# Cross-channel attention on one core: ten instead of eight batches loaded turned, with their loads and the small products placed anew

## What is computed

```python
rgb = jnp.transpose(rgb_emb, (0, 2, 1))      # x:   16 batches of 128 channels x 1024 positions
geo = jnp.transpose(geo_emb, (0, 2, 1))      # ctx: the same
scale = d ** (-0.5)                          # 8 heads of d = 16
def heads(x, w):
    return (x @ w.T).reshape(b, n, H, d).transpose(0, 2, 1, 3)
def xca(q, k, v):
    attn = jax.nn.softmax(jnp.einsum('bhni,bhnj->bhij', q, k) * scale, axis=-1)
    out = jnp.einsum('bhnd,bhde->bhne', v, attn)
    return out.transpose(0, 2, 1, 3).reshape(b, n, c)
res_p2r = xca(heads(rgb, wq_rgb), heads(geo, wk_point), heads(geo, wv_point)) @ proj_p2r.T
res_r2p = xca(heads(geo, wq_point), heads(rgb, wk_rgb), heads(rgb, wv_rgb)) @ proj_r2p.T
return jnp.transpose(rgb + res_p2r, (0, 2, 1)) + jnp.transpose(geo + res_r2p, (0, 2, 1))
```

## Time and profile before

| what | value |
|---|---|
| time, median of 3 runs | 140.67 us (140.2 to 141.71) |
| the profiled execution | 139.92 us, of which 137.9 us are the span of the trace |
| PE busy | 123.4 us (90%) |
| ACT busy | 86.1 us (62%) |
| POOL busy | 77.2 us (56%) |
| DVE busy | 71.3 us (52%) |
| moved by DMA | 34.25 MB |

### The profile page before, as it was taken

How to read it: one execution, slowest core, us unless ns; L and a number is a source line. 1 busy time by engine, 2 the same in 40 slices (tenths; PEclk the granted TensorE clock), 3 DMA queues, 4 the chain that set the end, 5 groups by cost and what they waited for, 6 DMA issues and landing times.

```text
span 137.9 us, 2676 instructions
## 1 busy us (share of the span) xinstructions
PE 123.4 (90%) x858; PEld 111.4 (81%) x858; DVE 71.3 (52%) x210; ACT 86.1 (62%) x194; POOL 77.2 (56%) x41
## 2 busy tenths in 40 slices
PE   7959879969992599999999999999999999979790
PEld 7838879868982598989898989898989898958560
DVE  0124255757750058696358696258696255353310
ACT  3133867765873427786967786967785967785341
POOL 5000668593756320959581959581959581959000
PEclk9999999999999689999999999999999999999999
DMA  4799999999999999999999999999603030300334
GB/s 138 250 373 417 283 226 232 227 277 288 259 349 378 367 349 322 249 209 312 421 374 341 316 206 353 412 411 415 247 12 152 5 152 0 157 0 0 152 155 152
DMA packets 16349, 34.25 MB, mean 248 GB/s; under 512 B 1360, under 2 KB 9680, under 8 KB 16336
## 3 DMA queue, kind: packets, MB, share of 16 engines
q1 hardware_dynamic: 13072, 30.94, 70.6%
q10 hardware_dynamic: 3264, 3.15, 8.2%
HBM read 25.69 MB, written 8.39 MB: 247 GB/s over the span
## 4 chain that ended last, share of the span: by engine, by line
PE 69%; DMA 17%; ACT 3%; DVE 2%; SPq 2%; issue 2%; POOL 2%; ACTq 0%; DVEq 0%
PE out_ps L299 24%; PE gram_bank L279 19%; DMA g_raw<-in_ctx_dram 17%; PE sy_bank L332 5%; PE gt_ps L258 5%; PE xt_ps L258 4%; PE t_bank L343 3%; PE sy_bank L359 2%; PE t_bank L344 2%; PE sy_bank L358 2%; ACT expd L407 2%; POOL x_lo L194 2%; PE uv_bank L322 1%; PE uv_bank L324 1%; PE uv_bank L323 1%
## 5 line engine op out<-in xcount | busy, mean ns | idle before, releaser
L194 POOL TENSOR_TENSOR x_lo<-x_raw,x_hi 128x1024 fp32r<-128x1024 f32 x16 | 38.0, 2374 | 45.0 <-ACT x_hi L375 45.0
L197 POOL TENSOR_TENSOR g_lo<-g_raw,g_hi 128x1024 fp32r<-128x1024 f32 x16 | 37.9, 2371 | 4.6 <-ACT g_hi L375 4.6
L279 PE MATMUL gram_bank<-gt,xt 128*128 128x128 f32 x256 | 34.4, 278 | 0.0
L279 PEld LDWEIGHTS gram_bank<-gt,xt 128*128 128x128 f32 x256 | 31.8, 195 | 0.0
L382 ACT COPY out_sb<-out_ps 128x512 f32<-128x512 f32 x32 | 18.6, 580 | 4.6 <-PE out_ps L299 3.1
L465 DVE COPY gt<-gt_ps 128x512 f32<-128x512 f32 x16 | 11.0, 688 | 14.6 <-PE gt_ps L258 14.6
L509 DVE COPY y_sb<-sy_bank 128x256 f32<-128x256 f32 x16 | 6.7, 421 | 22.8 <-PE sy_bank L332 22.8
L437 ACT CAST t_hi<-t_bank 128x256 fp32r<-128x256 f32 x16 | 6.0, 372 | 20.0 <-DVE t_bank L516 20.0
L407 ACT ACTIVATE expd<-scores,min_neg 128x128 f32<-128x128 f32 x32 | 12.6, 396 | 8.6 <-DVE min_neg L478 8.6
L375 ACT CAST g_hi<-g_raw 128x1024 fp32r<-128x1024 f32 x16 | 16.9, 1055 | 0.0
L375 ACT CAST x_hi<-x_raw 128x1024 fp32r<-128x1024 f32 x16 | 16.6, 1036 | 0.0
(11 more groups left out here) (49 smaller groups left out, 205.8 us busy)
## 6 DMA issues: line engine op xcount, KB each, us to landing
x_raw<-in_x_dram SPq DMA_DIRECT2D x15, 512.0 KB, 14.4
g_raw<-in_ctx_dram SPq DMA_DIRECT2D x15, 512.0 KB, 14.9
out_dram<-out_sb SPq DMA_DIRECT2D x15, 512.0 KB, 13.4
xz<-in_x_dram SPq DMA_DIRECT2D x10, 256.0 KB, 12.4
gz<-in_ctx_dram SPq DMA_DIRECT2D x10, 256.0 KB, 13.3
xz<-in_x_dram ACTq DMA_DIRECT2D x6, 256.0 KB, 15.5
gz<-in_ctx_dram ACTq DMA_DIRECT2D x6, 256.0 KB, 13.4
x_raw<-in_x_dram SPq DMA_DIRECT2D x2, 256.0 KB, 3.8
```

The costliest lines, as they stand in the source:

```text
L194: nc.gpsimd.tensor_tensor(x_lo[:, slot, :], x_raw[:, raw_slot, :], x_hi[:, slot, :].bitcast(F32), ALU.subtract).then_inc(x_lo_ready, 1)
L197: nc.gpsimd.tensor_tensor(g_lo[:, slot, :], g_raw[:, raw_slot, :], g_hi[:, slot, :].bitcast(F32), ALU.subtract).then_inc(g_lo_ready, 1)
L279: last = nc.tensor.matmul(gram_ps, xt[:, b % 2, cols], gt[:, b % 2, cols], start=(t == 0), stop=(t == TILES - 1))
```

## The change

- `VECTOR_PAIRS` becomes five pairs: batches 5 to 8 and 10 to 15 are loaded turned, ten instead of eight. PE turns batches 0 to 4 and 9 (six instead of eight).
- Loads at the start: ctx of batch 0 is issued by ACT; SP issues the plain load of batch 4 ahead of the first pair, and of the first pair only quads 0 and 1. Batch 5 comes ahead of the second pair.
- ACT issues quads 2 and 3 of x in one step and those of ctx in the next, in place of all four in one step; that now holds for the first pair too.
- In steps in which PE turns a batch, UV stands behind the transposes of half 0 where there is no output product yet, Y behind the first half of the Gram product, T behind the transposes of half 1; `copy_gt` of half 0 stands ahead of `y_sb` on DVE, and `copy_xt` of half 1 ahead of `t_hi` on ACT.

The core of the diff:

```diff
-VECTOR_PAIRS = ((4, 5), (7, 8), (10, 11), (13, 14))
+VECTOR_PAIRS = ((5, 6), (7, 8), (10, 11), (12, 13), (14, 15))
@@ SP, start
-            sp.dma_start(g_raw[:, 0, first], ctx[0][:, first]).then_inc(g_first, 16)
-            sp.dma_start(g_raw[:, 0, second], ctx[0][:, second]).then_inc(g_loaded[0], 16)
...
-            load_turned(sp, x_turn, xz, xz_loaded, 0, (0, 2, 1, 3))
-            load_turned(sp, g_turn, gz, gz_loaded, 0, (0, 2, 1, 3))
             load_plain(4)
+            load_turned(sp, x_turn, xz, xz_loaded, 0, (0, 1))
+            load_turned(sp, g_turn, gz, gz_loaded, 0, (0, 1))
+            load_plain(5)
             load_turned(sp, x_turn, xz, xz_loaded, 1, (0, 1))
             load_turned(sp, g_turn, gz, gz_loaded, 1, (0, 1))
-            load_plain(5)
@@ PE, step i
-                if 0 <= s < B:
+                if 0 <= s < B and l >= 0:
+                    uv_product(s)
                 if i in on_tensor:
                     turn_half(i, 0)
+                if 0 <= s < B and l < 0:
+                    uv_product(s)
+                if 0 <= y < B and i not in on_tensor:
+                    y_product(y)
...
                 if 0 <= g < B:
                     gram_half(g, 0)
+                if 0 <= y < B and i in on_tensor:
+                    y_product(y)
+                if i in on_tensor:
+                    turn_half(i, 1)
@@ ACT
+            nc.scalar.dma_start(g_raw[:, 0, first], ctx[0][:, first]).then_inc(g_first, 16)
+            nc.scalar.dma_start(g_raw[:, 0, second], ctx[0][:, second]).then_inc(g_loaded[0], 16)
-            issued_in = {3 if pair < PAIRS else VECTOR_PAIRS[pair - PAIRS][1] + 1: pair
-                         for pair in range(1, len(VECTOR_PAIRS))}
+            issued_in = {2 + 2 * pair if pair < PAIRS else VECTOR_PAIRS[pair - PAIRS][1] + 1: pair
+                         for pair in range(len(VECTOR_PAIRS))}
...
+                x_pair, g_pair = issued_in.get(i), issued_in.get(i - 1)
```

More of the change, by code:

```diff
@@ L167, in x_turned_half @@
                 eng.wait_ge(xt_copied, 2 * on_tensor.index(b) + 1 + half)
+        first, second = slice(0, HALF), slice(HALF, N)
         def plain_loaded(eng, b, loaded):
@@ L209, in store @@
                 sp.dma_start(out[b], out_sb[:, b % OUT_SLOTS, :]).then_inc(out_stored[b % OUT_SLOTS], 16)
-            first, second = slice(0, HALF), slice(HALF, N)
             sp.dma_start(x_raw[:, 0, first], x[0][:, first]).then_inc(x_first, 16)
-            sp.dma_start(g_raw[:, 0, first], ctx[0][:, first]).then_inc(g_first, 16)
             sp.dma_start(x_raw[:, 0, second], x[0][:, second]).then_inc(x_loaded[0], 16)
-            sp.dma_start(g_raw[:, 0, second], ctx[0][:, second]).then_inc(g_loaded[0], 16)
             load_plain(1)
@@ L302, in last_parts, with uv_product, y_product @@
                     last.then_inc(half_done, 1)
+            def uv_product(s):
+                pe.wait_ge(gram_lo_ready, s + 1)
+                if s == 0:
+                    pe.wait_ge(wu_lo_ready, 1)
+                else:
+                    pe.wait_ge(uv_copied, s)
+                nc.tensor.matmul(uv_ps, gram_hi[:, :], wu_hi[:, :, :], start=True, stop=False)
+                nc.tensor.matmul(uv_ps, gram_hi[:, :], wu_lo[:, :, :], start=False, stop=False)
+                nc.tensor.matmul(uv_ps, gram_lo[:, :], wu_hi[:, :, :], start=False, stop=True).then_inc(uv_done, 1)
+            def y_product(y):
+                if y >= 1:
+                    pe.wait_ge(y_copied, y)
+                pe.wait_ge(probs_ready, y + 1)
+                for a, wv in enumerate((WVP, WVR)):
+                    last = nc.tensor.matmul(y_ps[:, a * P:(a + 1) * P], probs[:, a, :], w_sb[:, wv, :],
+                                            start=True, stop=True)
+                last.then_inc(y_done, 1)
             pe.wait_ge(warm_ready, 1)
@@ L347, in _ @@
                     last_parts(B - 2, 1, 3, 6)
-                if i in on_tensor:
-                    turn_half(i, 1)
                 if 0 <= g < B:
@@ L388, in copy_xt @@
                 nc.scalar.copy(xt[:, b % 2, half * HALF:(half + 1) * HALF], xt_ps[:, :]).then_inc(xt_copied, 1)
-            issued_in = {3 if pair < PAIRS else VECTOR_PAIRS[pair - PAIRS][1] + 1: pair
-                         for pair in range(1, len(VECTOR_PAIRS))}
+            nc.scalar.dma_start(g_raw[:, 0, first], ctx[0][:, first]).then_inc(g_first, 16)
+            nc.scalar.dma_start(g_raw[:, 0, second], ctx[0][:, second]).then_inc(g_loaded[0], 16)
+            issued_in = {2 + 2 * pair if pair < PAIRS else VECTOR_PAIRS[pair - PAIRS][1] + 1: pair
+                         for pair in range(len(VECTOR_PAIRS))}
             for i in range(B + 4):
                 s, y, l = i - 2, i - 3, i - 4
-                pair = issued_in.get(i)
+                x_pair, g_pair = issued_in.get(i), issued_in.get(i - 1)
                 if 0 <= s < B:
@@ L411, in _ @@
                     split_hi(s, x_raw, x_loaded, x_hi, x_hi_ready)
[L412 to L415, removed]
+                if x_pair is not None:
+                    if x_pair >= PAIRS:
+                        pair_turned(act, x_pair - PAIRS)
+                    load_turned(act, x_turn, xz, xz_loaded, x_pair, (2,))
+                if g_pair is not None:
+                    load_turned(act, g_turn, gz, gz_loaded, g_pair, (2,))
                 if l >= 0:
                     evacuate(l, 0)
-                if pair is not None:
-                    load_turned(act, g_turn, gz, gz_loaded, pair, (2,))
                 if l >= 0 and l not in (B - 3, B - 2):
@@ L428, in _ @@
                     copy_xt(i, 0)
-                if pair is not None:
-                    load_turned(act, x_turn, xz, xz_loaded, pair, (3,))
                 if 0 <= s < B:
                     split_hi(s, g_raw, g_loaded, g_hi, g_hi_ready)
+                if x_pair is not None:
+                    load_turned(act, x_turn, xz, xz_loaded, x_pair, (3,))
+                if g_pair is not None:
+                    load_turned(act, g_turn, gz, gz_loaded, g_pair, (3,))
+                if i in on_tensor:
+                    copy_xt(i, 1)
                 if 0 <= y < B:
@@ L439, in _ @@
                     evacuate(l, 1)
[L440 to L443, removed]
                 if i == 1:
@@ L504, in _ @@
                     turn_half(i, 1, xz, xz_loaded, xt, xt_turned)
+                if i in on_tensor:
+                    copy_gt(i, 0)
                 if small_on:
@@ L511, in _ @@
                     turn_half(i, 1, gz, gz_loaded, gt, gt_ready)
-                if i in on_tensor:
-                    copy_gt(i, 0)
                 if small_on:
```

## The result

The changed kernel takes **145.7 us** (median of 4 runs, 144.1 to 146.99) against 140.87 us of the kernel before beside it (4 runs, 140.2 to 141.71): ratio 1.030, 95% interval 1.019 to 1.041. It is 4.8 us slower. The forecast was 142.5 us: the direction came and so did the mechanism (a late fifth pair), 3.2 us too small.

What follows compares the result with a forecast made beforehand. DMA and PE are both full for the first 97 us, PE alone after. Landing 105.2 + 1.7 + 31.5 = 138.4 us, plus 1.3 for the clock: 139.7 us of span, 142.5 us on the median; range 136.5 to 146 us.

Steps and rivals of the forecast that it cites:

- PE's work: On PE, two batches fewer are turned: 2 x 1.76 = 3.5 us less.
- The long wait of step 6: PE's wait for a plain ctx load, about 4.6 us, and the 1.56 us of half clock behind it go.
- UV, Y and T: Moved products cover waits of `uv_bank` and `t_bank`: worth nothing where DMA sets the pace, up to 2.6 us elsewhere.
- When the fifth pair lands: Last quad of `gz`, needed in step 14, lands at 96.9 + 8.8 - 0.5 = 105.2 us.
- ACT's issues a step later: Quads 2 and 3 of ctx, issued in step 13: taken as nothing, 4 us kept for the range.
- My first rival: Quads run side by side and the DMA keeps up: a pair costs 6.0 us, time 136.2 us; chance 27%.
- The rival of ACT's late issues: ACT's last ctx quad, in at 109.7 us, sets the end: time 146.9 us; chance 13%.
- 512 bytes: Skill's least transfer for line rate: by it a pair of turned loads costs 5.1 us, time 135.3 us.
- From landing to T: In step 14, PE's T starts 1.7 us after `gz` lands, `y_sb` standing behind two transposes on DVE.
- From T to the end: From step 14's T to the end: 33.2 us before, 1.76 less without batch 15's transposes, so 31.5 us.
- The clock's term: PE's clock falls after its wait for the fifth pair: 1.3 us, bounds 0 and 1.6.

## Why the prediction was right and wrong

- *PE's work*: right. From three to four pairs the span fell by 4.0 us (132.8 - 128.8); two batches at 1.76 are 3.5 (the medians fell by 3.0, on two chips).
- *The long wait of step 6*: right, gone. *UV, Y and T*: right, nothing here. Together they were put at 4.6 + 1.56 + 2.6 = 8.8 us wherever the DMA doesn't pace, and the kernel with four spaced pairs gained 9.1 us of span with all of them. I didn't take them singly, so the match is no proof for each.
- *When the fifth pair lands*, 105.2 us: with ACT's issues in one step 103.1 and 105.3, but partly by luck. The sum took the eighth store's issue (83.02 us) and the landing time (13.4 us) from the kernel before. In the changed kernel that store was issued at 78.43 us and took 23.1, so what stands ahead of the pair was in at 101.5 us, not at 96.9 - 0.5 = 96.4. With one step it was issued at 73.77 and took 22.6: 96.4, two errors that cancel. The pair itself landed 7.3 us behind the store (6.7 and 7.1 with one step) in place of 8.8. So the late landing is 5.1 us of what stood ahead, less 1.5 us of the pair.
- *ACT's issues a step later: "I take nothing"*: this is the step that failed, a term put at nothing. The pair landed at 108.8 us, and with the issues in one step the median was 3.4 us lower, no different from the kernel before (ratio 1.005). I looked at when each of ACT's quads would be in, one by one, and kept 4 us of range for that. What they cost is rate, from the first pairs on: SP's turned loads alone passed at 201 GB/s, with ACT's beside them at 334. My first rival even took the spreading for a reason that both queues would run side by side more; they did less.
- *The rival of ACT's late issues*, 146.9 us, came nearest to the time of this profile, by another way: ACT's queue was empty from 103 us on and SP's was last.
- *512 bytes*: the prediction set 227 GB/s against the Trainium skill's rule and took the rule for broken. These runs don't break it: 1 KB pieces over 128 partitions ran at 385 GB/s. The row was right and its cause was another, so a price near the row was still the right choice.
- *From landing to T*: 1.7 us, right. *From T to the end*: 34.4 us in place of 31.5. The clock's term was 1.3 us and measured 2.9: the five groups behind the wait took 0.80 + 0.43 + 1.71 + 0.43 + 0.43 us, and the output product 3.69 in place of 2.79. The wait, 5.7 us in one piece for PE, was longer than the 2.5 and 1.4 us from which I took the price, and the half clock lasted through a whole step's small products.

The two misses add up: 139.7 + 3.6 (landing) + 1.6 (clock) = 144.9 us, the span of this trace. That is 5.2 us; the miss of the median is only 3.2, since this execution was 1.3 us above the changed kernel's median and the one that the forecast was built on 0.75 below its own.

## What to carry to other kernels

A load into a quarter of the partitions cost the DMA nearly as much as one of twice its bytes (227 GB/s against 412), unless another queue filled the other half at the same moment (298 to 350 GB/s). Count such loads double, and place the two queues' issues side by side rather than in order of need. Where DMA and PE are both nearly full, look for waits on the double loads before adding one: four pairs with one batch between them waited for none and took 132.1 us, four in twos waited and took 139.1, five 144 to 146. Spacing alone isn't shown to be the reason. ACT's issues differ too between the first two (worth 3.4 us with five pairs), and the kernel before, spaced in the same way, took 140 us, for it lost 4.6 us to late plain loads in step 6 and 1.56 us to the clock behind them. Scatter between runs is no safe sign that the DMA paces a kernel: the three pairs scattered by 0.4 us and the kernel before by 11.5, but the four spaced pairs, also without a wait for a turned load, by 2.8 and the changed kernel by 2.4 to 2.9.

## What the runs showed of the hardware

- The DMA engines' busy share says nothing of the rate: 1.10 at 283 GB/s and 1.08 at 385 GB/s in the same stretch of two kernels, 1.13 at 227 and 1.03 at 412 in the kernel before.
- Two queues help each other only when they fill different halves of the partitions: 298 and 319 GB/s against 219 on the same half, with 227 for one queue alone.
- A stretch in which narrow and wide loads pass together can be slower than either alone. From 101 to 105 us the changed kernel (its repeat) moved 179 GB/s, where narrow loads alone manage 227 and plain ones 412:

```profile
DMA packets 343, 0.72 MB, mean 179 GB/s; under 512 B 31, under 2 KB 214, under 8 KB 343
q1 hardware_dynamic: 337, 0.71, 108.6%
```

- A wait and its clock: behind a PE wait of 5.7 us a step's small products ran at 1.2 GHz and the step took 2.9 us longer; behind waits of 2.5 and 1.4 us the clock cost 1.56 us.
- Issuing isn't free when the queue is full: SP stood 8.84 us at the two `xz` issues of the fifth pair, which held back its two `gz` issues and the plain load of batch 15:

```profile
79.71 8.84 SPq L154 DMA_DIRECT2D xz<-in_x_dram  x2
88.59 4.89 SPq L154 DMA_DIRECT2D gz<-in_ctx_dram  x2
93.61 3.72 SPq L206 DMA_DIRECT2D x_raw<-in_x_dram  x1
```
